# Reordering the second half of an attention and the distances behind it, token norms and root products on GpSimd, and row copies dealt out anew, in a decoder kernel on one Trainium2 core

## The chip, the cores and the metric

The kernel runs as one program on 1 core of a Trainium2 chip (trn2). The metric is device time in microseconds (us), the median of the timed runs. The engines are TensorE (PE in the profile), VectorE (DVE), ScalarE (ACT), GpSimd (POOL) and SyncE (SP), which only issues DMAs here.

## The reference

Two decoder layers over `x` of 8 sequences x 112 tokens x 256, with a context of 8 x 375 x 256. Each layer is self-attention, a cross step and a mixture of experts, each on a layer norm of `x` and added to it. The change lies in the first two steps of layer 0:

```python
x = x + _L0_attn_ref(_layernorm(x, axis=-1), Wk, Wq, Wv)     # causal, one head
x = x + _L0_xattn_ref(ctx_1024, _layernorm(x, axis=-1))
# in _L0_xattn_ref, for each of the 8 sequences (a: 375 context rows, b: 112 tokens):
#   D = sqrt(maximum(aa + bb - 2 * a @ b.T, 0))      aa, bb: sums of squares
#   R = dynamic time warping cost of D:  r = d + min(up, left, diagonal)
#   then the path is traced back through R, and the context rows on it are added to each token
```

## The kernel before

There is no scheduler: five instruction streams are written out by hand, one for each engine, and they meet in semaphores. T is 112 tokens, S 375 context rows, B 8 sequences; "pair q" is the sequences 2q and 2q+1, "half h" the sequences 4h to 4h+3. PSUM banks are handed out by a ring in the order of the `ring.take` calls, so a step can start only when the last reader of its bank has emptied it.

- **Attention, second half.** `shifted_scores(1)` on VectorE, `exp_rows(1, 0, 4)` on ScalarE (L1000), `weights_turned(1)` on TensorE (four transposes, L1216), `weights_moved(1)` on VectorE (L1818), `self_values(1)` on TensorE (L1213), `values_added(2)` and `(3)` on VectorE (L1826), which also take the statistics of the next layer norm. `ln_root` on GpSimd makes the reciprocal deviation `rstd` (L754, L755), `ln_norm(1, q)` on VectorE the normed tokens `N` (L1773).
- **What the distances need.** `ctx_turn(lo, hi)` on TensorE transposes the context into 12 banks, and `ctx_turned` on ScalarE copies them out (`ctxT_r`, L945). `pair_turn(turn1[q], 1, q)` transposes the normed tokens of a pair, `pair_turned` copies them out times -2 (`NT`, L945). `row_squares(q)` on ScalarE squares the normed tokens and sums them: `bb`, the token norms (L1014). The context norms lie in `root`.
- **Distances.** `distances(q)`: 4 products a sequence pair into two banks (`ps<-ctxT_r,NT`). `squares(lo, hi)` on VectorE adds the norms and empties the bank (L1837). `inverse_roots(lo, hi)` on ScalarE takes Relu, Ln and Exp(-0.5 x) (L1019 to L1021). `roots(n, lo, hi)` on VectorE (L1843 to L1845) takes the product z = d r and one Newton step, and signals `dist_ready`. There are five such groups n: sequences 0-1, 2-3, 4-5, 6 and 7.
- **Skewed copies.** The distances lie as [token, sequence, context column]; the recurrence wants them on 32 partitions, (g, b), where g is a quarter of the context columns. One DMA `skewed(b, g, k) <- plain_rows(b, g, k)` moves, for one sequence b and quarter g, the token rows of block k: rows 0-15 (k = 0), 16-47 (k = 1), 48-111 (k = 2), so 16, 32 or 64 rows of some 94 numbers. These are 96 DMAs, dealt by `mover` to the queues of SP (51, L627), ScalarE (19, L1058) and GpSimd (26, L797). Each waits for `dist_ready` of its sequence. GpSimd first clears the corners of the target (L780, L781: `dsk_clear`, for which SP and ScalarE wait), issues two loads of projection weights (`Wk`, `Wv`, L786), and clears the first cost rows (L791).
- **The recurrence.** 124 columns on VectorE, each with two scans (L1906) and two minima (L1901), with a shuffle (L1927) every third column. Before column q = 1, 5, 9 and 13 it waits for the first rows (k = 0) of quarter g = 0, 1, 2, 3 of all sequences, before column 17 for all of k = 1, before column 49 for all of k = 2. All that follows (path, experts, layer 1) hangs on its end.

## Time and profile before

| | |
|---|---|
| median of the 3 runs | 613.0 us (612.25 to 638.85) |
| profiled execution, its own time | 613.88 us |
| its span | 612.1 us |
| busy: PE, DVE, ACT, POOL | 469.0, 404.0, 222.1, 190.4 us |
| mean granted TensorE clock | 0.876 |

The span is what the rows below cover; the profiled execution's own time is 1.8 us longer. Times in rows are microseconds from the start of the span. An engine can be busy for most of the span and yet bound only some stages; so what counts is the chain of waits, stage by stage.

### The profile page before, as it was taken

The page shows a single profiled execution, that of the slowest core. Times are in us where ns is not written, and L with a number is a line of the kernel's source. Part 1 is how long each engine was busy: PE and PEld are TensorE (multiplying, and loading weights), DVE is VectorE, ACT ScalarE, POOL GpSimd, SP SyncE. Part 2 cuts the span into 40 slices and gives each one's busy share as a digit, 9 for nine tenths or more (in the row PEclk, how much of TensorE's full clock was granted, in tenths as well). Part 3 has the DMA queues.
Part 4 walks back from the last instruction along what each step waited for, and adds up shares of the span by engine and source line. Part 5 has one row for each costly group of instructions (what it writes and reads, how often), then busy time and mean ns, then how long its engine had stood idle before and what let it go on. Part 6 is the DMA issues. An engine that isn't in the chain of part 4 may idle for free.

```text
span 612.1 us, 9072 instructions
## 1 busy us (share of the span) xinstructions
PE 469.0 (77%) x2796; PEld 380.1 (62%) x2796; DVE 404.0 (66%) x1389; ACT 222.1 (36%) x670; POOL 190.4 (31%) x274
## 2 busy tenths in 40 slices
PE   7987799300030878799999989899998998799980
PEld 6975348200010346789999877788786775699850
DVE  6648569999899974715444376767764445756553
ACT  2546442200002324133444131779983353044300
POOL 6012630400000003156575227301103220377353
PEclk9988799755556899699999999979999996799995
DMA  9420298493100585222212230410007201155723
GB/s 231 85 90 2 54 52 36 92 110 64 18 0 5 170 303 169 91 71 70 69 60 63 75 82 0 123 52 2 2 1 222 88 2 60 35 150 169 130 84 114
DMA packets 49170, 50.43 MB, mean 82 GB/s; under 512 B 14768, under 2 KB 42052, under 8 KB 48900
## 3 DMA queue, kind: packets, MB, share of 16 engines
q1 hardware_dynamic: 40532, 34.53, 23.9%
q0 software_dynamic: 7824, 15.16, 11.4%
q8 instruction: 23, 0.38, 0.3%
q10 hardware_dynamic: 768, 0.18, 0.2%
q14 instruction: 23, 0.19, 0.1%
HBM read 37.48 MB, written 9.32 MB: 76 GB/s over the span
## 4 chain that ended last, share of the span: by engine, by line
PE 56%; DVE 26%; ACT 6%; DMA 4%; issue 3%; POOL 3%; ACTq 1%; POOLq 0%; DVEq 0%; SPq 0%
PE ps L1213 48%; DVE big L1906 8%; PE ps L1216 7%; DVE mtmp L1901 4%; POOL big L927 2%; DMA big<-Vc_r 2%; DVE big L2259 1%; ACT N_r L975 1%; ACTq L1058 1%; DVE rk L2251 1%; DVE big L1950 1%; DVE big L1951 1%; ACT big L945 1%; DVE big L1984 1%; DMA big<-in_L_attn_wo 1%
## 5 line engine op out<-in xcount | busy, mean ns | idle before, releaser
L1213 PE MATMUL ps<-ident 128*128 128x128 f32 (+1 forms) x304 | 63.0, 371 | 83.8 <-DVE big L1942 65.8
L1213 PEld LDWEIGHTS ps<-ident 128*128 128x128 f32 x304 | 45.4, 231 | 91.7 <-DVE big L1942 66.2
L1213 PE MATMUL ps<-ctxT_r,big 128*128 128x128 f32 (+1 forms) x616 | 82.8, 284 | 2.6 <-issue 1.1
L1213 PEld LDWEIGHTS ps<-ctxT_r,big 128*128 128x128 f32 (+1 forms) x616 | 75.8, 191 | 6.6 <-issue 4.3
L1906 DVE TENSOR_TENSOR_SCAN big<-mtmp,big 32x47 f32<-32x47 f32 x248 | 62.6, 287 | 8.1 <-DMA big<-Vc_r 8.1
L1213 PE MATMUL ps<-big 112*128 112x112 f32 (+6 forms) x458 | 63.2, 318 | 3.7 <-issue 3.4
L945 ACT ACTIVATE big<-ps 112x448 f32<-112x448 f32 (+6 forms) x65 | 38.2, 621 | 56.0 <-PE ps L1216 33.6
L1213 PEld LDWEIGHTS ps<-big 112*128 112x128 f32 (+5 forms) x458 | 53.0, 192 | 7.7 <-issue 4.4
L1216 PE MATMUL ps<-ident,big 112*112 112x112 f32 (+6 forms) x291 | 42.3, 285 | 13.0 <-DVE big L1984 4.4
L945 ACT ACTIVATE ctxT_r<-ps 128x256 f32<-128x256 f32 (+3 forms) x74 | 31.0, 433 | 57.2 <-PE ps L1216 47.0
L1216 PEld LDWEIGHTS ps<-ident,big 112*112 112x112 f32 (+6 forms) x291 | 32.3, 148 | 27.5 <-DVE big L1984 10.2
L1146 ACT ACTIVATE big<-ps,rk 112x112 f32<-112x112 f32 x128 | 43.9, 375 | 8.5 <-DVE rk L2252 8.0
L1213 PE MATMUL ps<-big,ctxT_r 128*128 x168 | 39.6, 380 | 0.0
L2194 DVE COPY big<-ps 128x256 f32<-128x256 f32 x21 | 8.9, 425 | 43.8 <-PE ps L1213 41.2
L918 POOL DMA_INDIRECT ctxT_r<-normed,source x29 | 32.5, 1119 | 15.6 <-PE ps L1216 8.8
L1901 DVE TENSOR_TENSOR mtmp<-big 32x47 f32<-32x47 f32 x246 | 37.1, 183 | 0.0
L754 POOL TENSOR_SCALAR veps<-mv 112x2 f32<-112x2 f32 x24 | 5.7, 238 | 99.2 <-DVE mv L1767 98.9
L1120 ACT ACTIVATE ctxT_r<-ps,big 128x128 f32<-128x128 f32 x84 | 23.9, 368 | 30.6 <-PE ps L1213 30.6
L1078 ACT ACTIVATE big<-big,ones 112x1500 f32<-112x1500 f32 x2 | 3.1, 1538 | 82.5 <-DVE big L1958 82.5
L1213 PEld LDWEIGHTS ps<-big,ctxT_r 128*128 128x128 f32 x168 | 30.4, 191 | 3.3
L846 POOL DMA_INDIRECT ctxT_r<-normed,source x21 | 25.5, 1217 | 21.0 <-PE ps L1216 12.9
L2251 DVE TENSOR_REDUCE rk<-ps 112x4 f32<-112x448 f32 x32 | 19.8, 620 | 17.2 <-PE ps L1213 17.2
(266 smaller groups left out, 941.5 us busy)
## 6 DMA issues: line engine op xcount, KB each, us to landing
big<-in_L_ffn_W SPq DMA_DIRECT2D x16, 512.0 KB, 6.9
routed<-Vc_r SPq DMA_DIRECT2D x29, 128.0 KB, 2.5
ctxT_r<-in_ctx POOLq DMA_DIRECT2D x4, 750.0 KB, 21.4
big<-in_ctx SPq DMA_DIRECT2D x4, 672.0 KB
big<-in_L_ffn_Wg SPq DMA_DIRECT2D x16, 128.0 KB, 2.5
big<-in_L_ffn_Wu SPq DMA_DIRECT2D x16, 128.0 KB, 2.6
big<-in_L_ffn_Wd SPq DMA_DIRECT2D x16, 128.0 KB, 2.5
normed<-N_r SPq DMA_DIRECT2D x2, 896.0 KB, 5.2
```

The lines of the kernel that those rows point to most:

```text
L846: pool.indirect_dma_start(out=Xg0[:, n % XR], out_offset=None, in_=normed0, in_offset=bass.IndirectOffsetOnAxis(ap=source[:, n:n + 1], axi ...
L918: pool.indirect_dma_start(out=Xg[:, n % XR], out_offset=None, in_=normed, in_offset=bass.IndirectOffsetOnAxis(ap=source[:, n:n + 1], axis= ...
L927: pool.indirect_dma_start(out=Yg[:, k * B + b], out_offset=None, in_=routed, in_offset=bass.IndirectOffsetOnAxis(ap=slot_id[:, k * B + b:k ...
L945: return nc.scalar.activation(dst, src, func, **kw).then_inc(free[act], 1)
L1120: ins = nc.scalar.activation(hT0[:, m % 2, j], src[:, j * 128:(j + 1) * 128], ACT.Relu, bias=b1t[:, j, m:m + 1])
L1146: ins = nc.scalar.activation(Px[:, n % NP, j * T:(j + 1) * T], bank(r_s1[n])[0:T, j * T:(j + 1) * T], ACT.Exp, bias=hm[:, n % NP, 1, j:j + ...
L1213: return nc.tensor.matmul(dst, lhsT, rhs, start=first, stop=last)
L1216: return nc.tensor.transpose(dst, src, ident[0:n, 0:n])
L1901: return step(v.tensor_tensor(mtmp[:, lo:hi], RS[:, q - 1, lo:hi], RS[:, q - 1, lo + 1:hi + 1], ALU.min))
L1906: return step(v.tensor_tensor_scan(RS[:, q, lo + 1:hi + 1], mtmp[:, lo:hi], Dsk[:, (q - 1) * RC + lo:(q - 1) * RC + hi], RS[:, q, lo:lo + ...
L2194: empty(r_y0[m], v.tensor_copy(yb0[:, m % YR], bank(r_y0[m])[:, 0:D]))
L2251: link(v.tensor_reduce(hm[:, n % NP, 0, :], src, AX_X, ALU.max))
```

## The change

It has four parts.

1. **Order** on TensorE and ScalarE (and the ring): the exponentials come ahead of two context copies; the context turns 4-5 and the turn of token pair 1 come ahead of the turned weights; token pairs 2 and 3 are turned ahead of `distances(2)` and `(3)`, which follow each other; `r_bias` goes last. On VectorE `squares(4, 6)` comes ahead of `roots(1, 2, 4)`.
2. **Token norms** `bb` are made on GpSimd as D x variance x rstd x rstd (three instructions on 112x2 a pair), in place of eight squares on ScalarE.
3. **Root product**: for groups n = 0, 1, 2 (`POOL_ROOTS = 3`) z = d r is one GpSimd instruction on 112x750; VectorE keeps the two others. ScalarE's Relu writes `Dd` in place.
4. **Copies**: a table `MOVES` deals the same 96 DMAs out as SP 53, GpSimd 31, ScalarE 12, in another order.

```diff
         MOVES = {
+            "sp": row_block(0, (0, 1), every) + row_block(0, (2, 3), every) + row_block(0, (4, 5), (0, 1))
+            + row_block(0, (6,), (0, 1)) + row_block(0, (7,), (0,)) + row_block(1, (4, 5), (1,))
+            + row_block(1, (6, 7), (0, 1)) + row_block(2, range(B), (0, 1, 2)),
...
+            "act": row_block(1, (2, 3), (0, 1)) + row_block(0, (7,), (1, 3)) + row_block(1, (2, 3), (2, 3))
+            + row_block(1, (4, 5), (0,))}
...
+            def row_squares(q4):
+
+                cols = slice(2 * q4, 2 * q4 + 2)
+                link(nc.gpsimd.tensor_scalar(bb[:, cols], mv[:, cols, 1], float(D), None, ALU.mult))
+                pool.wait_ge(s["rstd_ready"], B // 2 + q4 + 1)
+                link(nc.gpsimd.tensor_tensor(bb[:, cols], bb[:, cols], rstd[:, cols], ALU.mult))
+                nc.gpsimd.tensor_tensor(bb[:, cols], bb[:, cols], rstd[:, cols], ALU.mult).then_inc(s["bb_ready"], 1)
+
+            def first_product(n, lo, hi):
+                pool.wait_ge(s["inv_ready"], n + 1)
+                nc.gpsimd.tensor_tensor(root[:, lo:hi, :], Dd[:, lo:hi, :], inv[:, lo:hi, :], ALU.mult)\
+                    .then_inc(s["product_ready"], 1)
...
-            ln_root(1)
+            for q4 in range(B // 2):
+                ln_root(1, (q4,))
+                row_squares(q4)
+            if POOL_ROOTS:
+                first_product(0, 0, 2)
...
-            pool.wait_ge(s["bb_ready"], B)
...
+            for n in range(1, POOL_ROOTS):
+                first_product(n, 2 * n, 2 * n + 2)
+            for b, g, k in MOVES["pool"]:
...
             def roots(n, lo, hi):
                 d, r, z = Dd[:, lo:hi, :], inv[:, lo:hi, :], root[:, lo:hi, :]
-                ve.wait_ge(s["inv_ready"], n + 1)
-                link(v.scalar_tensor_tensor(z, d, 0.0, r, ALU.max, ALU.mult))
+                if n < POOL_ROOTS:
+                    ve.wait_ge(s["product_ready"], n + 1)
+                else:
+                    ve.wait_ge(s["inv_ready"], n + 1)
+                    link(v.tensor_tensor(z, d, r, ALU.mult))
```

On TensorE, from the turn of token pair 0 (`ident,N_r` is a turn of tokens, `ident,big` with 112x112 the turned weights and with 128x125 context turns, `ctxT_r,NT` a distance product, `big 112x256` the values). Before:

```order
L1216 MATMUL ps<-ident,N_r 128x112 x4
L1216 MATMUL ps<-ident,big 112x112 x4
L1216 MATMUL ps<-ident,big 128x125 x8
L1213 MATMUL ps<-ctxT_r,NT 112x375 x4
L1216 MATMUL ps<-ident,N_r 128x112 x4
L1213 MATMUL ps<-big 112x256 x4
L1213 MATMUL ps<-ctxT_r,NT 112x375 x4
L1216 MATMUL ps<-ident,big 128x125 x24
L1216 MATMUL ps<-ident,KcT_r 128x4
L1216 MATMUL ps<-ident,N_r 128x112 x4
L1213 MATMUL ps<-ctxT_r,NT 112x375 x4
L1216 MATMUL ps<-ident,N_r 128x112 x4
```

On the same engine from the same place, after the change:

```order
L1233 MATMUL ps<-ident,N_r 128x112 x4
L1233 MATMUL ps<-ident,big 128x125 x8
L1233 MATMUL ps<-ident,N_r 128x112 x4
L1233 MATMUL ps<-ident,big 112x112 x4
L1230 MATMUL ps<-ctxT_r,NT 112x375 x4
L1230 MATMUL ps<-big 112x256 x4
L1233 MATMUL ps<-ident,big 128x125 x16
L1230 MATMUL ps<-ctxT_r,NT 112x375 x4
L1233 MATMUL ps<-ident,N_r 128x112 x4
L1233 MATMUL ps<-ident,big 128x125 x8
L1233 MATMUL ps<-ident,N_r 128x112 x4
L1230 MATMUL ps<-ctxT_r,NT 112x375 x8
```

The last distances (the final x8) now stand behind both token turns in one piece, and nothing has to be turned and copied between them.

On GpSimd, from the last `rstd` of this layer norm to the first skewed copies. Before:

```order
L755 TENSOR_TENSOR rstd<-veps,mhalf 112x2
L780 MEMSET big 32x2x1128
L781 MEMSET big 32x100
L786 DMA N_r<-in_L_xattn_Wk 128x2x256
L786 DMA N_r<-in_L_xattn_Wv 128x2x256
L791 MEMSET big 32x475
L793 MEMSET big 8x1
L797 DMA big<-Vc_r 1x16x93 x8
```

And after the change:

```order
L763 TENSOR_TENSOR rstd<-veps,mhalf 112x2
L775 TENSOR_SCALAR bb<-mv 112x2
L777 TENSOR_TENSOR bb<-bb,rstd 112x2
L778 TENSOR_TENSOR bb<-bb,rstd 112x2
L782 TENSOR_TENSOR Vc_r<-Vc_r,big 112x750
L805 MEMSET big 32x2x1128
L806 MEMSET big 32x100
L810 DMA N_r<-in_L_xattn_Wk 128x2x256
L810 DMA N_r<-in_L_xattn_Wv 128x2x256
L815 MEMSET big 32x475
L817 MEMSET big 8x1
L782 TENSOR_TENSOR Vc_r<-Vc_r,big 112x750 x2
```

The first product stands ahead of the clearing of the copy's target, and the second and third behind the two loads and the clearing of the first cost rows; all of GpSimd's copies stand behind the third.

On the queue of SP, the skewed copies (a shape is sequences x rows x columns). Before:

```order
L627 DMA big<-Vc_r 1x16x94 x15
L627 DMA big<-Vc_r 1x32x94 x12
L627 DMA big<-Vc_r 1x64x94 x24
```

And after the change:

```order
L635 DMA big<-Vc_r 1x16x94 x6
L635 DMA big<-Vc_r 1x16x93 x2
L635 DMA big<-Vc_r 1x16x94 x6
L635 DMA big<-Vc_r 1x16x93 x2
L635 DMA big<-Vc_r 1x16x94 x7
L635 DMA big<-Vc_r 1x32x94 x6
L635 DMA big<-Vc_r 1x64x94 x24
```

SP now carries 23 copies of 16 rows and 6 of 32 rows ahead of the same 24 copies of 64 rows; the last of the 23 is sequence 7, quarter 0.

## Rows read from the trace of the kernel before

**Rows 1.** the page: its span, and the shares of the chain that ended last
```profile
span 612.1 us, 9072 instructions
...
PE 56%; DVE 26%; ACT 6%; DMA 4%; issue 3%; POOL 3%; ACTq 1%; POOLq 0%; DVEq 0%; SPq 0%
```

**Rows 2.** the chain of waits, 36 to 130 us: start, us, what
```profile
80.80 10.60 DMA big<-Vc_r
91.42 0.30 DVE big L1906
```

**Rows 3.** VectorE in order of time: start, us, instruction [idle before, what ended it]
```profile
47.12 0.88 DVE L1826 SCALAR_TENSOR_TENSOR X<-ps,rs,X 112x256 f32<-112x256 f32 x2 [0.64 <-PE ps L1213]
...
52.11 0.74 DVE L1773 TENSOR_SCALAR N_r<-X,mv,rstd 112x256 f32<-112x256 f32 x2 [0.60 <-POOL rstd L755]
...
54.77 0.94 DVE L1844 SCALAR_TENSOR_TENSOR big<-big,Vc_r 112x750 f32<-112x750 f32 x1
...
71.59 0.55 DVE L1845 SCALAR_TENSOR_TENSOR Vc_r<-big,Vc_r 112x375 f32<-112x375 f32 x1
...
75.72 0.30 DVE L1906 TENSOR_TENSOR_SCAN big<-mtmp,big 32x47 f32<-32x47 f32 x1 [3.47 <-DMA big<-Vc_r]
...
86.51 0.29 DVE L1906 TENSOR_TENSOR_SCAN big<-mtmp,big 32x47 f32<-32x47 f32 x1
```

**Rows 4.** TensorE in order of time, the same columns
```profile
40.31 2.66 PE L1216 MATMUL ps<-ident,big 112*112 112x112 f32 x12 [2.32 <-ACT big L1000]
...
50.30 2.73 PE L1216 MATMUL ps<-ident,big 125*128 125x125 f32 x24
...
57.09 4.44 PE L1213 MATMUL ps<-ctxT_r,NT 128*112 128x375 f32 x8 [2.55 <-ACT NT L945]
...
62.59 2.75 PE L1213 MATMUL ps<-ctxT_r,NT 128*112 128x375 f32 x8 [0.68 <-ACT NT L945]
```

**Rows 5.** a stretch: us, busy of each engine, granted clock (PEclk), DMA share, GB/s
```profile
58.00:59.00 1.00, 1.00 (x2) 0.37 (x2) 0.97 (x2) 0.00 (x0) 0.00 (x0) 0.50 0.06 12
```

**Rows 6.** ScalarE in order of time
```profile
48.34 0.92 ACT L1020 ACTIVATE big<-big,tiny 112x750 f32<-112x750 f32 x1
...
50.93 2.98 ACT L945 ACTIVATE ctxT_r<-ps 128x500 f32<-128x500 f32 x6 [0.81 <-PE ps L1216]
...
61.95 0.54 ACT L945 ACTIVATE NT<-ps 128x448 f32<-128x448 f32 x1 [4.17 <-PE ps L1216]
...
104.07 4.51 ACT L945 ACTIVATE Vc_r<-ps 125x512 f32<-125x512 f32 x9 [11.86 <-DMA big<-Vc_r]
```

**Rows 7.** GpSimd in order of time
```profile
53.09 1.97 POOL L780 MEMSET big<- 32x2256 f32 x1 [1.01 <-PE ps L1216]
...
64.61 0.72 POOL L786 DMA_DIRECT2D N_r<-in_L_xattn_Wv  x1
...
72.43 9.36 POOL L797 DMA_DIRECT2D big<-Vc_r  x19 [1.14 <-DVE Vc_r L1845]
```

**Rows 8.** GpSimd, groups by shape: busy us, mean ns of one
```profile
L866 POOL TENSOR_TENSOR X<-X,big 112x2048 f32<-112x2048 f32 x2 | 9.2, 4586 | 3.2 <-ACT N_r L975 3.2
L894 POOL TENSOR_TENSOR big<-big 128x448 f32<-128x448 f32 x8 | 7.4, 930 | 6.7 <-DVE big L2246 6.7
L852 POOL TENSOR_TENSOR ctxT_r_split<-big,ctxT_r_split 128x256 fp32r<-128x256 f32 x6 | 6.5, 1084 | 2.8 <-ACT ctxT_r_split L1125 2.7
```

**Rows 9.** SP's queue issuing DMAs, 56 to 63 us
```profile
56.77 5.69 SPq L627 DMA_DIRECT2D big<-Vc_r  x9
```

**Rows 10.** ScalarE's copies issued from 73.1 us, then from 79.5 us, and their landing
```profile
L1058 ACTq DMA_DIRECT2D big<-Vc_r x3: 600/600/616, 73.1 to 74.4; - x3
...
DMA to landing us min/median/max: 2.6/2.7/2.7
...
L1058 ACTq DMA_DIRECT2D big<-Vc_r x3: 601/603/608, 79.5 to 80.8; - x3
...
DMA to landing us min/median/max: 7.2/8.8/10.6
```

More of the change, by code:

```diff
@@ L527, in decoder_kernel @@
         first_rows_moved = [sem(f"first_cost_rows_moved{g}") for g in range(G)]
+        pool_first_rows_moved = [sem(f"first_cost_rows_moved_by_pool{g}") for g in range(G)]
         rows_moved = {k: sem(f"cost_rows_moved{k}") for k in range(1, NBLK)}
@@ L560, in plain_rows, with row_block, first_rows_in, pool_row_sem @@
             return bass.AP(src.tensor, src.offset, [src.ap[0], [1, min(RC, S - g * RC)]])
-        def mover(b, g, k):
-            if g == G - 1:
-                return "pool"
-            if k == 0:
-                return "act" if b in (3, 5, 7) else "sp"
-            if k == 1:
-                return ("sp", "sp" if b < HB else "act", "act" if b < B - 2 else "pool")[g]
-            return "sp"
-        def moved_by(queue, k):
-            pairs = [(b, g) for q4 in range(B // 2) for g in range(G) for b in (2 * q4, 2 * q4 + 1)]
-            return [(b, g) for b, g in pairs if mover(b, g, k) == queue]
+        def row_block(k, bs, gs):
+            return [(b, g, k) for g in gs for b in bs]
+        every = range(G)
+        MOVES = {
+            "sp": row_block(0, (0, 1), every) + row_block(0, (2, 3), every) + row_block(0, (4, 5), (0, 1))
+            + row_block(0, (6,), (0, 1)) + row_block(0, (7,), (0,)) + row_block(1, (4, 5), (1,))
+            + row_block(1, (6, 7), (0, 1)) + row_block(2, range(B), (0, 1, 2)),
+            "pool": row_block(1, (0, 1), every) + row_block(0, (4, 5), (2, 3)) + row_block(0, (6,), (2, 3))
+            + row_block(0, (7,), (2,)) + row_block(1, (4, 5), (2, 3)) + row_block(1, (6, 7), (2, 3))
+            + row_block(2, range(B), (3,)),
+            "act": row_block(1, (2, 3), (0, 1)) + row_block(0, (7,), (1, 3)) + row_block(1, (2, 3), (2, 3))
+            + row_block(1, (4, 5), (0,))}
+        assert sorted(sum(MOVES.values(), [])) == [(b, g, k) for b in range(B) for g in every for k in range(NBLK)]
         def rows_in(k):
-            n = len(moved_by("pool", k))
+            n = sum(move[2] == k for move in MOVES["pool"])
             return 16 * (G * B - n), 16 * n
+        def first_rows_in(g):
+            n = sum(move[1:] == (g, 0) for move in MOVES["pool"])
+            return 16 * (B - n), 16 * n
         def row_sem(k, g):
             return first_rows_moved[g] if k == 0 else rows_moved[k]
+        def pool_row_sem(k, g):
+            return pool_first_rows_moved[g] if k == 0 else pool_rows_moved[k]
         def step_of(seg, g):
@@ L623, in _ @@
             sp.wait_ge(s["dsk_clear"], 1)
-            for k in range(NBLK):
-                for b, g in moved_by("sp", k):
-                    sp.wait_ge(s["dist_ready"], max(b // 2, b - 3) + 1)
-                    sp.dma_start(skewed(b, g, k), plain_rows(b, g, k)).then_inc(row_sem(k, g), 16)
+            for b, g, k in MOVES["sp"]:
+                sp.wait_ge(s["dist_ready"], max(b // 2, b - 3) + 1)
+                sp.dma_start(skewed(b, g, k), plain_rows(b, g, k)).then_inc(row_sem(k, g), 16)
             sp.wait_ge(s["edge_ready"], 1)
@@ L1034, in _ @@
             norms_turned(1)
+            exp_rows(1, 0, 4)
             ctx_turned(2, 4)
             pair_turned(turn1[0], 0, scale=-2.0)
[L1037 to L1038 removed]
             ctx_turned(4, 6)
             pair_turned(turn1[1], 1, scale=-2.0)
[L1041 removed]
             inverse_roots(0, 2)
[L1043 to L1044 removed]
+            ctx_turned(6, 10)
+            pair_turned(turn1[2], 2, scale=-2.0)
+            ctx_turned(10, 12)
+            pair_turned(turn1[3], 3, scale=-2.0)
             inverse_roots(2, 4)
[L1046 to L1049 removed]
             inverse_roots(4, 6)
@@ L1052, in _ @@
             inverse_roots(7, 8)
+            copy(r_bias, bcol[:, :], bank(r_bias)[:, 0:NB])
             sc.wait_ge(s["dsk_clear"], 1)
-            for k in range(2):
-                for b, g in moved_by("act", k):
-                    sc.wait_ge(s["dist_ready"], max(b // 2, b - 3) + 1)
-                    sc.dma_start(skewed(b, g, k), plain_rows(b, g, k)).then_inc(row_sem(k, g), 16)
+            for b, g, k in MOVES["act"]:
+                sc.wait_ge(s["dist_ready"], max(b // 2, b - 3) + 1)
+                sc.dma_start(skewed(b, g, k), plain_rows(b, g, k)).then_inc(row_sem(k, g), 16)
             sc.wait_ge(free[act], r_bias.count)
@@ L1879, in _ @@
             roots(0, 0, 2)
+            squares(4, 6)
             roots(1, 2, 4)
-            squares(4, 6)
             squares(6, 7)
```

71 lines of the change are left out of this document (31 added, 40 removed).

## Prediction

> **What bounds the kernel now.** First the page's shares of the chain that ended last: TensorE 56%, VectorE 26% [rows 1]. This says nothing of the changed stage, so I read the chain of waits from 36 to 130 us. The change ends where the recurrence on VectorE begins. From there the chain is VectorE alone, column after column, with one hole: a copy issued at 80.80 us on ScalarE's queue lands 10.60 us later, at 91.4, and a scan starts with it [rows 2]. VectorE in order of time shows both debts of the old order. The last distance is done at 71.59 + 0.55 = 72.1, and the first scan starts at 75.72, 3.47 us idle behind a copy. Then 16 columns run until 86.51 + 0.29 = 86.8, and column 17 starts at 91.42: 4.62 us idle [rows 3, 2]. From 75.72 to 86.80, 16 columns take 11.08 us, 0.69 each. Behind column 17 nothing waits until column 49 and further: ScalarE's value copies, which wait for all blocks, went on at 104.07 [rows 6], and column 49 comes at 91.42 + 32 x 0.69 = 113.5. Whatever starts column 17 earlier therefore moves the rest of the kernel by as much; the later stages wait for each other and for loads that this chain releases.
>
> Before 72.1 the old order loses time in three places. TensorE waits 2.32 us for the exponentials and then runs its turns slowly (12 in 2.66 us, where 24 take 2.73 later) [rows 4]. It waits 2.55 us for a token copy and then takes 4.44 us for eight distance products, where the next eight take 2.75 [rows 4]: the granted clock there is 0.50 [rows 5]. And VectorE has nine root steps behind the last distance bank.
>
> **The change, laid end to end with those durations.** I start at 37.4, where nothing has moved yet.
>
> *Order.* ScalarE's two context copies and one token copy, 2 x 0.49 + 0.44 = 1.4 us [rows 6], no longer stand ahead of the exponentials, so these end at 38.9 instead of 40.3. TensorE meanwhile turns two context banks (0.46 each, 2.73 / 6 [rows 4]) and a token pair, until 39.2, and then the weights. Its idle of 2.32 shrinks to some 0.7 before distances(0), which start at 40.4 when ScalarE has made up the 1.4. With 2.8 a distance pair (2.75 [rows 4]) and 1.8 for the values: distances(0) end at 43.2, values 45.0, four context banks 46.8, distances(1) 49.7, token pair 2, two banks and pair 3 at 51.4, distances(2) and (3) together at 57.1. Before, the last ended at 62.59 + 2.75 = 65.3. The x update of pair 2 starts at 44.2 in place of 47.12, and the norm of pair 3 (52.11 before [rows 3]) at 49.05.
>
> *Norms.* Eight squares leave ScalarE. GpSimd gets 3 small instructions a pair, some 0.8 us with their links; for pairs 2 and 3 they end at 48.0 and 49.8, beside VectorE's work. The squares step needs them later: nothing.
>
> *Product.* No row shows a GpSimd product of 112x750. Two float32 ones give 930 / 448 = 2.1 and 4586 / 2048 = 2.2 ns an element, the one that rounds its output 1084 / 256 = 4.2 [rows 8]. So the bounds are 1.6 and 3.2 us; I take 1.65, the shape and type being those of the first two. It takes 0.94 (a VectorE step [rows 3]) off VectorE three times, 2.8 us, but GpSimd's line is in order. Product 0 runs 49.8 to 51.4; then the two clearings (1.97 [rows 7] and 0.28) to 53.65, which frees SP's copies; the two load issues (1.5, the second 0.72 [rows 7]) and the clearing of cost rows (0.67) to 55.8. The second root factor of ScalarE (three steps, 2.6 us, the middle one 0.92 [rows 6]) is ready at 54.6. So product 1 runs 55.8 to 57.5, over a second late, and VectorE stands idle for 2.7 us before its two steps: group 1 is done at 59.45. Product 2 runs 57.6 to 59.2 and delays nobody. VectorE: squares of 6 and 7 to 60.5, group 2 to 62.4, 3 to 64.1, 4 to 65.75. The last distance is thus done 6.4 us before 72.1.
>
> *Copies.* SP issues nine 16-row copies in 5.69 us, 0.632 each [rows 9]. Its first eight run from 53.65 to 58.7. The other eight of pairs 0 and 1 wait for group 1, 59.5; from there 14 stand ahead of (7, quarter 0), which is issued at 59.5 + 14 x 0.632 = 68.3, 2.6 us after its distance is ready. SP's queue, not VectorE, then starts the recurrence, and what sets SP is product 1. Before, ScalarE issued that copy at 73.1, and it landed after 2.6 [rows 10], at 75.7: the first scan. So now 68.3 + 2.6 = 70.9: **4.8 us earlier**.
>
> The second debt: the rows of k = 1 are issued by 72.1 on SP (6 behind 68.9), 70.2 on GpSimd, 70.1 on ScalarE, where the last one went out at 80.8. Copies issued from 73.1 landed in 2.6 to 2.7 us; those of 79.5 to 80.8 took 7.2 to 10.6 [rows 10]. Between lie GpSimd's 64-row copies: its 19 from 72.43 on are 11 shorter and then 8 of those [rows 7], so the first went at 77.85. SP's last one now goes 1.4 us after GpSimd's first of 64 rows (70.7); before, 1.65 us after it the price was 7.2. So it lands by 79.3. Column 17 comes at 70.9 + 11.1 = 82.0 and finds it there, with 2.7 us to spare: **4.6 us saved**. k = 2 is issued to 88.8 and at 10.6 us a landing lies there by 99, against column 49 at 104. ScalarE, free at 71.4 instead of 81.4, copies keys earlier; TensorE's key and value products ended well before the recurrence and are off the path.
>
> Sum: 4.8 + 4.6 = 9.4 us. SP and ScalarE will issue together from 63.7, with which I charge a single stall of 0.3, leaving 9.1. The profiled execution took 613.88 (a span of 612.1 and 1.8 around it), so 604.8; the median lies 0.9 lower: **603.9**.
>
> **The rivals.**
>
> *Product dear.* While product 2 runs, VectorE has its two steps of group 1 in hand, with both operands in the same memory. The Trainium skill ("SBUF — State Buffer", Who interferes with whom) holds that a VectorE instruction with two SBUF inputs and a GpSimd one that reads SBUF exclude each other, the second waiting for the whole of the first. No row here shows that; at 1.65 us it would cost 0.6 us at the last distance, all inside the 2.6 that SP is late, so the sum would be the same by rule or without. At 3.2 us a product with the two taking turns: product 0 puts 1.55 on all behind it, product 1 as much, and product 2, first in turn, holds VectorE's steps back 3.1 to 3.2 more. Group 1 is then 6.2 us later, SP with it, and 9.4 - 6.2 = 3.2 are left: 609.8. Without turns 5.1 - 6.0 are left. For it: 4.2 ns is on record for a GpSimd instruction. Against: the two of its own type. Chance 0.14.
>
> *The hole stays.* SP's last k = 1 copy may pay 10.6 or more instead of 7, since at that time GpSimd's eight 64-row copies and SP's own come behind each other closer than before. At 10.6 it lands at 82.7 and costs 0.7; if the whole hole stays, 4.8 are left, 608.2. Chance 0.12.
>
> *Slower than before.* One mechanism: the product on GpSimd, with turns. Each further us of product puts 3 to 4 us on group 1; 9.4 us are eaten at 3.2 + 3.2 / 3.5 = 4.1 us or a little above. At 5 us (6.7 ns an element) it would be 3 us slower, 616. No row of such shape comes near: 0.04.
>
> *It does not do what it says.* SP's queue of 53, or the copies of k = 2, hold column 49 in place of 17: it has 5 us of cover. If used up and more, 3 are lost: 607. Chance 0.05.
>
> *More gained.* With a product at 1.2, or clearings that start sooner, group 1 comes at 58.5 and the scan at 69.9: 10.4 saved, 602.6. To pass 2% (12.3 us) SP would have to be ready at 65, before the last distance. Chance 0.08, of which 0.03 beyond 2%.
>
> **How the numbers follow.** The forecast has 0.57 and spans 602.6 to 605.5, with half a microsecond either way for another run. The range takes in the dear product and the kept hole: 602.0 to 610.2. About 2% (12.3 us) is what a measurement of this kernel tells from no change. By the cases: faster by more 0.04, within 0.93, slower 0.03.
>
> **What would show it.** In the changed profile: distances in one piece of 16 products ending near 57 at full clock; a GpSimd row of 112x750 of some 1650 ns; VectorE idle some 2.7 us in front of its first step of group 1, waiting for GpSimd; the first scan near 71, released by a copy of SP's queue; no idle time before column 17 (near 82). It is wrong if the product is over 2 us, if VectorE's steps stretch beside it, or if column 17 or 49 waits for a copy.

## The result, and the profile after

The changed kernel takes **605.18 us** (median of 4 runs, 603.93 to 606.38), forecast 603.9. Beside it the kernel before took 612.25 and 613.0; two further runs of it (638.65 and 638.85) and some of most kernels below, among them the profiled ones of e3, e5 and e6, were in a slower state and are left out of every ratio. The ratio is 0.9878, 95% interval [0.9831, 0.9926]: some 7.4 us faster, less than 2% at its middle. The profiled execution took 604.03 us. The page of after, its span and the shares of the chain that ended last (TensorE down, VectorE up in share):

```profile
span 602.1 us, 9072 instructions
...
PE 49%; DVE 30%; POOL 5%; DMA 5%; ACT 5%; issue 4%; SPq 1%; POOLq 0%; DVEq 0%
```

The two profiled executions are not level where the change begins. In a stretch of 4 us (length, busy time of PE, granted clock, DMA share, GB/s), before:

```profile
12.00:16.00 4.00, 3.56 (x10) 0.60 1.12 232
```

and after:

```profile
12.00:16.00 4.00, 3.61 (x17) 1.00 1.11 238
```

TensorE had the lower of its two levels (1.2 of 2.4 GHz) for most of that stretch in before alone. To take differences ahead of the change out I count from **P**, the end of the norm of token pair 1 on VectorE, the last step that no kernel here moves. VectorE of before, that norm (P = 37.15 + 0.73 = 37.88) and the last scan of the recurrence:

```profile
37.15 0.73 DVE L1773 TENSOR_SCALAR N_r<-X,mv,rstd 112x256 f32<-112x256 f32 x2
...
165.44 0.30 DVE L1906 TENSOR_TENSOR_SCAN big<-mtmp,big 32x47 f32<-32x47 f32 x1
```

VectorE of after, in order of time (P = 36.47):

```profile
35.74 0.73 DVE L1791 TENSOR_SCALAR N_r<-X,mv,rstd 112x256 f32<-112x256 f32 x2
...
50.47 0.94 DVE L1865 SCALAR_TENSOR_TENSOR big<-big,Vc_r 112x750 f32<-112x750 f32 x1 [1.07 <-POOL Vc_r L782]
...
56.38 2.50 DVE L1865 SCALAR_TENSOR_TENSOR big<-big,Vc_r 112x750 f32<-112x750 f32 x1 [2.97 <-POOL Vc_r L782]
58.91 0.94 DVE L1866 SCALAR_TENSOR_TENSOR Vc_r<-big,Vc_r 112x750 f32<-112x750 f32 x1
...
65.41 0.55 DVE L1866 SCALAR_TENSOR_TENSOR Vc_r<-big,Vc_r 112x375 f32<-112x375 f32 x1
...
71.85 0.30 DVE L1927 TENSOR_TENSOR_SCAN big<-mtmp,big 32x47 f32<-32x47 f32 x1 [5.79 <-DMA big<-Vc_r]
...
156.91 0.30 DVE L1927 TENSOR_TENSOR_SCAN big<-mtmp,big 32x47 f32<-32x47 f32 x1
```

The last distance is done at P + 29.5 (P + 34.3 before), the first scan starts at P + 35.4 (P + 37.8 [rows 3]), the last at P + 120.4 (P + 127.6). From first to last scan it is 89.7 before and 85.1 after: the 4.62 us of [rows 2] are gone. So by these two executions the change is worth **7.1 us** at the end of the recurrence; the rest of the 10 us between the spans lies in other stages and in P. VectorE stood idle 2.97 us for product 1 and then took 2.50 us for a step that takes 0.94.

TensorE, GpSimd, and the chain of waits:

```profile
38.93 2.75 PE L1230 MATMUL ps<-ctxT_r,NT 128*112 128x375 f32 x8 [0.76 <-ACT NT L970]
...
49.10 5.21 PE L1230 MATMUL ps<-ctxT_r,NT 128*112 128x375 f32 x16
```

```profile
48.65 1.79 POOL L782 TENSOR_TENSOR Vc_r<-Vc_r,big 112x750 f32<-112x750 f32 x1
50.38 1.97 POOL L805 MEMSET big<- 32x2256 f32 x1
...
54.59 3.49 POOL L782 TENSOR_TENSOR Vc_r<-Vc_r,big 112x750 f32<-112x750 f32 x2
...
66.25 8.41 POOL L822 DMA_DIRECT2D big<-Vc_r  x17 [0.35 <-DVE Vc_r L1866]
```

```profile
68.16 0.61 SPq L635
68.81 3.02 DMA big<-Vc_r
```

TensorE's idle of 2.32 is down to 0.76, and the 4.44 us for eight products [rows 4] are gone; distances 2 and 3 are one piece at full clock. Products take 1.75 to 1.79 us. Product 1 and product 2 stand back to back in one row, 54.59 to 58.08. The first scan waits for SP's queue: (7, quarter 0), its 23rd copy, was issued at 68.81, 2.85 us behind the last distance. GpSimd's 17 copies from 66.25 on are nine shorter ones and then eight of 64 rows, the first of these at 70.7.

Counting from P doesn't take out everything. In before the granted clock fell once more behind P; here are the 2 us in which the first turns ran (same columns as above):

```profile
40.00:42.00 2.00, 1.69 (x9) 0.53 0.81 279
```

These twelve turns took 2.66 us [rows 4]. The kernel of e1 below has the same instructions in the same order up to the last distance, and the same idle time in front; at a granted clock of 1.00 it took

```profile
38.84 1.45 PE L1223 MATMUL ps<-ident,big 112*112 112x112 f32 x12 [2.32 <-ACT big L1006]
```

With the eight products behind (3.06 and 2.69 us) this makes the 1.6 us by which its last distance comes earlier (P + 32.7). So up to 1.6 us of the 4.8 at the last distance, and with it of the 7.1, belong to one execution's clock and not to the change. The 4.44 us are another matter: behind an idle time of 2.56 us (2.55 before) the eight products took 4.25 in e1 too, with a granted clock of 0.50 from 56 to 58 us; that loss goes with the old order; in the changed kernel the clock stays at 1.00 from 36 to 60 us.

### The profile page after: what moved, and what is told of

Read it like the earlier page. It is cut to its first block, busy times and chain, and to the rows that moved or that the text cites. A ratio compares the mean times of both kernels' runs of the same rounds, so it can differ in the third digit from the quotient of the medians.

```text
span 602.1 us, 9072 instructions
## 1 busy us (share of the span) xinstructions
PE 458.8 (76%) x2796; PEld 371.8 (62%) x2796; DVE 402.8 (67%) x1386; ACT 218.8 (36%) x654; POOL 201.6 (33%) x294
## 4 chain that ended last, share of the span: by engine, by line
PE 49%; DVE 30%; POOL 5%; DMA 5%; ACT 5%; issue 4%; SPq 1%; POOLq 0%; DVEq 0%
PE ps L1230 43%; DVE big L1927 9%; PE ps L1233 7%; DVE mtmp L1922 4%; POOL big L952 2%; DVE big L2283 1%; DVE rk L2275 1%; ACT N_r L1000 1%; DVE big L1974 1%; DVE big L1975 1%; ACT big L970 1%; DMA big<-in_L_attn_wo 1%; DVE big L2008 1%; DMA big<-scattered 1%; DVE big L1951 1%
## 5 line engine op out<-in xcount | busy, mean ns | idle before, releaser
L1230 PE MATMUL ps<-ident 128*128 128x128 f32 (+1 forms) x304 | 60.6, 361 | 76.6 <-DVE big L1966 58.4
L1230 PEld LDWEIGHTS ps<-ident 128*128 128x128 f32 x304 | 43.3, 221 | 84.4 <-DVE big L1966 58.8
L1230 PE MATMUL ps<-big 112*128 112x112 f32 (+6 forms) x458 | 60.4, 308 | 3.7 <-issue 3.4
L970 ACT ACTIVATE big<-ps 112x448 f32<-112x448 f32 (+6 forms) x65 | 38.6, 627 | 54.3 <-PE ps L1233 34.3
L1230 PEld LDWEIGHTS ps<-big 112*128 112x128 f32 (+5 forms) x458 | 50.8, 184 | 7.8 <-issue 4.3
L970 ACT ACTIVATE ctxT_r<-ps 128x256 f32<-128x256 f32 (+3 forms) x74 | 31.1, 432 | 52.5 <-PE ps L1233 25.9
L1233 PE MATMUL ps<-ident,big 112*112 112x112 f32 (+6 forms) x291 | 40.6, 275 | 11.7 <-DVE big L2008 4.4
L1233 PEld LDWEIGHTS ps<-ident,big 112*112 112x112 f32 (+6 forms) x291 | 30.7, 143 | 25.7 <-DVE big L2008 10.2
L1000 ACT ACTIVATE N_r<-X,shift,rstd 112x256 f32<-112x256 f32 x32 | 17.4, 592 | 36.0 <-POOL shift L769 36.0
```

Of the source, the lines that this page charges most:

```text
L970: return nc.scalar.activation(dst, src, func, **kw).then_inc(free[act], 1)
L1000: nc.scalar.activation(N[:, b, :], X[:, b, :], ACT.Identity, bias=shift[:, b:b + 1], scale=rstd[:, b:b + 1]).then_inc(s["norm_ready"], 1)
L1230: return nc.tensor.matmul(dst, lhsT, rhs, start=first, stop=last)
L1233: return nc.tensor.transpose(dst, src, ident[0:n, 0:n])
```

## The experiments

All read in one table. Times are P + the number, each from one profiled execution; landing is that of (7, quarter 0) after its issue; "hole" is idle time before column 17. The ratio is to before on the same chip; its intervals are 2 to 6 us either way, and every one of them overlaps the changed kernel's (those of e2 and e10 barely), so the times don't rank these kernels. The traces repeat better: kernels with the same work up to the last distance have it within 0.3 us (changed and e7; e4, e5, e8 and e11), the 1.6 us between before and e1 apart. And in all fourteen traces the last scan comes 85.0 to 85.2 us behind the first, plus the hole. So only two numbers have to be explained, the first scan and the hole. From 36 to 60 us the mean granted clock was 0.87 in before, 0.93 in e1 and e6, and 0.99 or 1.00 in all others.

| kernel | last distance | (7, q0) issued, landing | first scan | hole | last scan | ratio, 95% |
|---|---|---|---|---|---|---|
| before | 34.3 | 35.2, 2.6 | 37.8 | 4.6 | 127.6 | 1 |
| changed | 29.5 | 32.3, 3.0 | 35.4 | 0 | 120.4 | 0.9878 [0.9831, 0.9926] |
| e1_copies_only | 32.7 | 34.2, 2.8 | 37.0 | 0 | 122.1 | 0.9869 [0.9773, 0.9965] |
| e2_copies_undone | 29.5 | 30.6, 3.0 | 33.6 | 4.3 | 123.0 | 0.9961 [0.9917, 1.0005] |
| e3_product2_later | 28.9 | 31.3, 3.1 | 34.4 | 0 | 119.5 | 0.9870 [0.9835, 0.9905] |
| e4_one_product | 26.8 | 31.6, 6.4 | 38.0 | 0 | 123.0 | 0.9899 [0.9843, 0.9954] |
| e5_hold_big | 26.6 | 31.1, 2.6 | 33.7 | 0 | 118.7 | 0.9874 [0.9829, 0.9919] |
| e6_norms_back | 30.8 | 33.6, 3.0 | 36.7 | 0 | 121.7 | 0.9909 [0.9879, 0.9939] |
| e7_sp_order | 29.2 | 29.4, 2.2 | 31.6 | 3.0 | 119.7 | 0.9915 [0.9879, 0.9951] |
| e8_best | 26.8 | 28.2, 2.7 | 30.9 | 0 | 115.9 | 0.9860 [0.9810, 0.9909] |
| e9_order_only | 27.6 | 27.8, 1.9 | 29.8 | 4.5 | 119.3 | 0.9906 [0.9855, 0.9957] |
| e10_norms_back_guarded | 29.2 | 32.0, 2.8 | 34.8 | 0 | 119.8 | 0.9967 [0.9919, 1.0016] |
| e11_front | 26.8 | 26.9, 2.1 | 29.0 | 0 | 114.1 | 0.9815 [0.9747, 0.9883] |
| e12_products_back | 26.6 | 30.3, 2.8 | 33.1 | 1.8 | 120.0 | 0.9936 [0.9889, 0.9982] |

### e1_copies_only: the kernel before with the new table

```diff
-            for k in range(NBLK):
-                for b, g in moved_by("sp", k):
...
+            for b, g, k in MOVES["sp"]:
```

(Part of the edit; the same for the queues of GpSimd and ScalarE, and the table)

> The old order, norms and roots, with the new table of copies alone. All times are counted from P, the end of the norm of token pair 1 on VectorE (37.88 us in the profile before, 36.47 in that of the change), so that a slower or faster start does not count. Before: first scan at P + 37.8, column 17 at P + 53.5, last scan at P + 127.6. Changed: P + 35.4, P + 46.5, P + 120.4, that is 7.1 us earlier. Theory (two separate debts): copies alone do not move the first scan by more than 0.6 us (it needs the last distance and, after it, one copy), but close the hole before column 17: idle there below 0.3 us in place of 4.6, last scan at P + 122.6 to 123, 607.5 to 608.5 us in all. Rival (the hole closes only because the order frees ScalarE early and SP can start early): idle before column 17 stays at 2 us or more, and the total within 2 us of before.

The chain and VectorE at the first scan:

```profile
70.66 2.79 DMA big<-Vc_r
```

```profile
73.47 0.30 DVE L1913 TENSOR_TENSOR_SCAN big<-mtmp,big 32x47 f32<-32x47 f32 x1 [4.24 <-DMA big<-Vc_r]
```

The hole is gone, and the last scan comes 5.5 us earlier than before: 4.6 of the hole and 0.8 at the first scan, more than the 0.6 allowed for, where the last distance came 1.6 us earlier by the clock. The table by itself closes the hole.

### e2_copies_undone: the changed kernel with the old dealing

```diff
-            for b, g, k in MOVES["sp"]:
+            for k in range(NBLK):
+                for b, g in moved_by("sp", k):
```

(Part of the edit; the same for the queues of GpSimd and ScalarE)

> The changed kernel with the old table of copies (SP 51, GpSimd 26, ScalarE 19). Theory: the first scan comes at P + 33.5 to 34.5, a little sooner than the P + 35.4 of the change, since sequence 7's first copy is then 7th on ScalarE's queue, free at 63.9 us; but the hole before column 17 is back with 4 to 6 us, because ScalarE's last 32-row copy goes out 3.5 us behind GpSimd's first 64-row one. Last scan P + 123.5 to 125, total 3 to 4.5 us slower than the change, 608 to 610. Rival (the order alone is what helps): no hole, total as the change or 1 us faster.

ScalarE, and VectorE in order of time:

```profile
64.92 0.52 ACT L1032 ACTIVATE Vc_r<-Vc_r 112x375 f32<-112x375 f32 x1 [4.30 <-DVE Vc_r L1848]
```

```profile
60.90 2.50 DVE L1858 SCALAR_TENSOR_TENSOR big<-big,Vc_r 112x750 f32<-112x750 f32 x1 [2.96 <-POOL Vc_r L775]
...
74.61 0.30 DVE L1920 TENSOR_TENSOR_SCAN big<-mtmp,big 32x47 f32<-32x47 f32 x1 [4.02 <-DMA big<-Vc_r]
...
89.98 0.30 DVE L1920 TENSOR_TENSOR_SCAN big<-mtmp,big 32x47 f32<-32x47 f32 x1 [4.29 <-DMA big<-Vc_r]
```

The hole is back with 4.29 us, and the last scan is 2.6 us later than in the changed kernel, although the first is 1.8 us earlier. The 2.50 us step is there again.

### e3_product2_later: product 2 only behind group 1

```diff
             for n in range(1, POOL_ROOTS):
+                if n == 2:
+                    pool.wait_ge(s["dist_ready"], 2)
                 first_product(n, 2 * n, 2 * n + 2)
```

> The changed kernel, with one wait more: GpSimd takes the third product only when the distances of group 1 are done. Theory (VectorE and GpSimd exclude each other while both read two operands): in the profile of the change VectorE's first step of group 1 took 2.50 us in place of 0.94, beside product 2; here it takes 0.94, group 1 is done 1.5 us earlier, and so are SP's copy of sequence 7, the first scan (P + 33.9) and the last scan (P + 118.9): 1.5 us faster than the change, though product 2 itself comes 1.9 us later. Rival (the 2.50 is something else, such as a late hand-over or DMA work of GpSimd): the step stays over 2 us, and the total does not move or is slower.

```profile
57.34 0.94 DVE L1867 SCALAR_TENSOR_TENSOR big<-big,Vc_r 112x750 f32<-112x750 f32 x1 [2.94 <-POOL Vc_r L782]
```

With nothing else on GpSimd the same step takes 0.94 in place of 2.50 (so it does in e4, at 55.61), and group 1 is done at P + 21.8 in place of P + 23.4. At the first scan 1.0 of these 1.6 us is left: the first of SP's copies behind group 1 (59.3) took 0.9 us in place of 0.6, and the landing and GpSimd's line did not move with it. So product 2 beside VectorE's step costs about 1 us at the end of the recurrence; the times, 0.9870 and 0.9878, don't show it.

### e4_one_product: `POOL_ROOTS = 1`

```diff
-        POOL_ROOTS = 3
+        POOL_ROOTS = 1
```

> The changed kernel with one root product on GpSimd in place of three (POOL_ROOTS = 1): groups 1 and 2 take their product on VectorE. Theory (product 1 came late because it stands behind clearings and loads on GpSimd): VectorE has group 1 done at 56.3 in place of 59.9, SP's copy of sequence 7 goes out 3.5 us earlier, at about 65, right behind the last distance at 63.7; first scan P + 31.5 to 32, last scan P + 117, 3.5 us faster than the change, 601.5 us. Rival (taking 0.94 us three times off VectorE is what makes the change fast): the last distance comes later than the 65.9 of the change and the kernel is slower by 1 to 2 us.

The chain, and GpSimd:

```profile
69.36 6.36 DMA big<-Vc_r
```

```profile
64.90 8.42 POOL L822 DMA_DIRECT2D big<-Vc_r  x17 [0.35 <-DVE Vc_r L1866]
```

The last distance comes 2.7 us earlier, and the first scan 2.6 us **later**. My expectation of the issue was also wrong in its sum: SP had 22 copies of 0.63 ahead of (7, quarter 0), from 53.9 on and without a pause, which is 67.8, and one of them took 1.6. It came at 69.36, just as GpSimd's first 64-row copy went (64.90 + 9 x 0.495 = 69.35), and then landed after 6.36 us.

### e5_hold_big: e4 with the 64-row copies held

```diff
-        POOL_ROOTS = 3
+        POOL_ROOTS = 1
...
+            held = True
...
+                if k == 2 and held:
+                    pool.wait_ge(first_rows_moved[0], first_rows_in(0)[0])
+                    held = False
```

> The kernel with one GpSimd product, in which GpSimd also holds its copies of k = 2 (64 rows each) until the first rows of quarter 0 have all landed. It is compared with the one-product kernel, whose first scan stood at P + 38.0 and last scan at P + 123.0 (P: the end of the norm of token pair 1 on VectorE), and where the copy of (7, quarter 0) was issued at P + 31.6 and landed after 6.36 us. Theory (GpSimd's 64-row copies in flight stretched that landing): it lands after 2.6 to 3.2 us, the first scan stands at about P + 34.5, the last at about P + 119.5, 3.4 us earlier than there; of times, about 602.5. Rival (the landing is long because SP's own 22 copies were issued without a pause ahead of it): it stays over 5 us and the first scan within 1 us of P + 38.

```profile
68.89 2.58 DMA big<-Vc_r
```

The landing is 2.58 us, and the last scan 4.3 us earlier than in e4 (of 3.4 expected). So GpSimd's 64-row copies in flight stretched the landing, and not SP's own line.

### e6_norms_back: token norms on ScalarE again

```diff
-                row_squares(q4)
...
+            pool.wait_ge(s["bb_ready"], B)
...
+            row_squares(0)
```

> The changed kernel with the token norms on ScalarE as before (eight squares with a sum; GpSimd waits for all of them ahead of its two loads), all else as changed. Theory (ScalarE has 1.1 and 4.3 us idle in that stage, and the three small GpSimd instructions a pair cost GpSimd's line 0.8 us ahead of product 0): no more than 0.8 us either way, first scan at P + 34.6 to P + 36, so that the move of the norms is worth nothing by itself. Rival (ScalarE's second and third root factors come later by its squares, four of 0.4 us): the group-1 step comes 1.6 us or more later, first scan at P + 37, and the time is 1.6 us or more above the changed kernel.

VectorE, GpSimd and TensorE in order of time:

```profile
49.50 4.01 DVE L1793 TENSOR_SCALAR N_r<-X,mv,rstd 112x256 f32<-112x256 f32 x1 [0.60 <-POOL rstd L763]
```

```profile
49.43 1.81 POOL L774 TENSOR_TENSOR Vc_r<-Vc_r,big 112x750 f32<-112x750 f32 x1
51.17 1.97 POOL L796 MEMSET big<- 32x2256 f32 x1
```

```profile
53.97 0.57 PE L1235 MATMUL ps<-ident,N_r 112*128 112x112 f32 x4 [3.19 <-DVE N_r L1793]
```

1.3 us later at the last scan than the changed kernel, beyond the 0.8 of the theory; but not by the rival's mechanism. The norm of one sequence of pair 3 took 4.01 us, where such a norm takes 0.4: it began 0.07 behind product 0 and ended 0.37 behind the clearing. TensorE waited 3.19 us for it, and behind that wait its granted clock was 0.50 (56 to 58 us) and distances 2 and 3 took 6.90 us in place of 5.21. In the changed kernel the three small norm instructions put product 0 at 48.65, 0.3 us behind the last of these norms (48.36).

### e7_sp_order: SP's list by readiness

```diff
-            "sp": row_block(0, (0, 1), every) + row_block(0, (2, 3), every) + row_block(0, (4, 5), (0, 1))
-            + row_block(0, (6,), (0, 1)) + row_block(0, (7,), (0,)) + row_block(1, (4, 5), (1,))
+            "sp": row_block(0, (0, 1), every) + row_block(0, (2, 3), (0, 1)) + row_block(0, (2,), (2,))
+            + row_block(0, (4, 5), (0,)) + row_block(0, (3,), (2,)) + row_block(0, (6,), (0,)) + row_block(0, (2,), (3,))
+            + row_block(0, (7,), (0,)) + row_block(0, (4, 5), (1,)) + row_block(0, (6,), (1,)) + row_block(0, (3,), (3,))
+            + row_block(1, (4, 5), (1,))
```

> The changed kernel with nothing but SP's list in another order: the 16-row copies of quarter 0 go as soon as their distance is there, (7, quarter 0) right at the last distance instead of behind 14 copies that are ready with group 1, and the copies of quarters 1 to 3 fill in between and behind. Same copies on the same queues. Theory (SP's line in front of (7, quarter 0) sets the first scan): it is issued at P + 29.6 to 30, lands after 2.6, first scan at about P + 32.4 (changed kernel: P + 35.4), last scan at about P + 117.5; with column 17 at P + 43.5 and the last copy of k = 1 landed by P + 42.5. About 3 us faster than the changed kernel, 602. Rival 1 (the last distance or something else sets it): first scan within 1 us of P + 35.4. Rival 2 (the end of k = 1 is late in its place): idle time before column 17 of 1 to 3 us and no gain at the last scan.

```profile
72.23 9.78 DMA big<-Vc_r
```

```profile
82.04 0.30 DVE L1929 TENSOR_TENSOR_SCAN big<-mtmp,big 32x47 f32<-32x47 f32 x1 [3.00 <-DMA big<-Vc_r]
```

The first scan comes 3.8 us earlier, so SP's line did set it. Then rival 2: SP's last copy of k = 1, issued at 72.23 among the 64-row copies, lands after 9.78, and column 17 waits 3.00. Of 3.8 us 0.7 is left, not the 3 expected; the ratio, 0.9915, shows no gain at all.

### e8_best: one product, and a table for both terms

```diff
+            "pool": row_block(1, (0, 1), every) + row_block(0, (2, 3), (3,)) + row_block(1, (2, 3), (2, 3))
+            + row_block(0, (4, 5), (2, 3)) + row_block(0, (6,), (2, 3)) + row_block(0, (7,), (2,))
+            + row_block(1, (4, 5), (2, 3)) + row_block(1, (6, 7), (2, 3)) + row_block(2, range(B), (3,)),
+            "act": row_block(1, (2, 3), (0, 1)) + row_block(1, (4, 5), (0,)) + row_block(0, (7,), (1, 3))
+            + row_block(1, (6, 7), (1,))}
```

(Part of the edit; with `POOL_ROOTS = 1`. SP's list is that of e11, below, with the two copies of quarter 2 ahead of (7, quarter 0).)

> One GpSimd product (last distance 2.7 us earlier than in the changed kernel) and a new table of copies: SP's list in the order in which distances come ready, some copies of quarters 1 to 3 given from SP to ScalarE and GpSimd. Theory (both terms together, SP's line and GpSimd's 64-row copies in flight, set the first scan): (7, quarter 0) is issued at P + 27.6, first scan at about P + 30.5, last scan at about P + 115.5, 5 us faster than the changed kernel, about 600. Rival (the copies then come so close that k = 1 lands late): idle time of over 1 us in front of column 17, and a last scan at P + 117 or later.

```profile
65.91 2.68 DMA big<-Vc_r
```

No hole, last scan at P + 115.9: 4.5 us earlier than the changed kernel. SP's last copy of k = 1 is issued at 70.4 here, 0.2 us behind GpSimd's first 64-row copy, and lands in 4.5.

### e9_order_only: the new order and nothing else

```diff
-        POOL_ROOTS = 3
+        POOL_ROOTS = 0
...
-            for b, g, k in MOVES["sp"]:
+            for k in range(NBLK):
+                for b, g in moved_by("sp", k):
```

(Part of the edit, against the changed kernel; the other queues in the same way, and the norms on ScalarE as in e6. Of part 3 it keeps that Relu writes `Dd` in place and that VectorE's product is a `tensor_tensor`.)

> The new order of the second half alone: token norms on ScalarE, all root products on VectorE and the copies as before. To be read beside the kernel before (last distance P + 34.3, first scan P + 37.8, last scan P + 127.6; P is the end of the norm of token pair 1) and beside the changed kernel with the old copies (P + 29.5, P + 33.6, P + 123.0). Theory (of what the change wins ahead of the copies, all is the order; moving the product and the norms to GpSimd adds nothing): last distance at P + 27 to P + 28, first scan at P + 31 to P + 32.5, the hole before column 17 still there with 4 to 6 us, last scan at P + 121 to P + 123. Rival (ScalarE's squares hold up the root factors, so that the norms on GpSimd are what lets the order pay): last distance at P + 29.5 or later and the last scan at P + 124 or later.

ScalarE, and VectorE:

```profile
58.76 0.52 ACT L1030 ACTIVATE Vc_r<-Vc_r 112x375 f32<-112x375 f32 x1 [0.94 <-DVE Vc_r L1850]
```

```profile
67.41 0.30 DVE L1922 TENSOR_TENSOR_SCAN big<-mtmp,big 32x47 f32<-32x47 f32 x1 [2.01 <-DMA big<-Vc_r]
...
82.96 0.30 DVE L1922 TENSOR_TENSOR_SCAN big<-mtmp,big 32x47 f32<-32x47 f32 x1 [4.46 <-DMA big<-Vc_r]
```

The order alone starts the recurrence 8.1 us earlier and ends it 8.2 us earlier than before (up to 1.6 us of either by the clock in before's trace), 1.1 us **ahead of the whole change**, with the hole still in it. That is better than I expected. Beside e2, which adds the products and norms on GpSimd, it starts 3.9 us earlier. That is the price of those moves together, with the old dealing: ScalarE waits 4.30 us in e2, and 0.94 here, for the squares that stand behind group 1 on VectorE; its own copies, (7, quarter 0) its seventh, then start at P + 26.8 in place of P + 24.0, and (7, quarter 0) lands in 3.0 in place of 1.9. (Order alone ahead of the whole change is read from one execution of each; the ratios, 0.9906 and 0.9878, don't part them.)

### e10_norms_back_guarded: e6, and product 0 behind the norms

```diff
+                pool.wait_ge(s["norm_ready"], 2 * B)
                 first_product(0, 0, 2)
```

(Part of the edit; the rest is e6's edit)

> The kernel with the norms back on ScalarE, and one more wait: GpSimd starts product 0 only when VectorE has normalised token pair 3. Without it the first of these two norms took 4.01 us (0.40 elsewhere) beside GpSimd's product 0 (1.81) and clearing (1.97), and the first scan stood at P + 36.65. Theory (that norm and GpSimd's instructions exclude each other, which is what made the norms on ScalarE dearer): the norm takes 0.4 again, TensorE's distances 2 and 3 run in one piece of 5.2 us, and the first scan stands at P + 35 to P + 35.8, as in the changed kernel. Rival (the 1.3 us come from ScalarE's squares): the norm takes 0.4, the first scan stays at P + 36.3 or later.

VectorE, and GpSimd:

```profile
48.49 0.74 DVE L1794 TENSOR_SCALAR N_r<-X,mv,rstd 112x256 f32<-112x256 f32 x2 [0.60 <-POOL rstd L763]
...
57.99 2.40 DVE L1869 SCALAR_TENSOR_TENSOR Vc_r<-big,Vc_r 112x750 f32<-112x750 f32 x1
```

```profile
57.62 1.97 POOL L774 TENSOR_TENSOR Vc_r<-Vc_r,big 112x750 f32<-112x750 f32 x1 [0.64 <-ACT big L1039]
```

A wait added makes it 1.9 us faster than e6 in the trace (first and last scan alike): both norms take 0.74 together. The stretched step is now the other one of group 1, 2.40, since product 2 starts later. It starts at 57.62, while VectorE's first step (57.02, 0.94 us) still runs, and is stretched itself, to 1.97. The times don't repeat the gain: they point the other way (0.9967 beside 0.9909, on different chips, with intervals that overlap). So the mechanism rests on the rows, and that the kernel as a whole gains is not shown.

### e11_front: e8 with (7, quarter 0) first of all

```diff
-            + row_block(0, (2,), (2,)) + row_block(0, (6,), (0,)) + row_block(0, (3,), (2,)) + row_block(0, (7,), (0,))
-            + row_block(0, (4, 5), (1,)) + row_block(0, (6,), (1,)) + row_block(1, (4, 5), (1,))
+            + row_block(0, (6,), (0,)) + row_block(0, (7,), (0,))
+            + row_block(0, (4, 5), (1,)) + row_block(0, (6,), (1,)) + row_block(0, (2, 3), (2,)) + row_block(1, (4, 5), (1,))
```

> The kernel with one product and the new table (first scan P + 30.86, last scan P + 115.9; its copy of (7, quarter 0) was SP's 18th, issued 1.3 us after the last distance behind two copies of quarter 2), with these two copies of quarter 2 moved behind the quarters 0 and 1. Theory (what stands ahead of (7, quarter 0) on SP still sets the first scan): it is issued at P + 26.9, first scan at P + 29.6, last scan at P + 114.6, 1.3 us faster, about 601 us. Rival (quarter 2 is late for column 9, or a long landing): idle time of 0.5 us or more before column 5, 9 or 17 and the last scan where it was.

```profile
65.63 2.13 DMA big<-Vc_r
```

```profile
67.78 0.30 DVE L1928 TENSOR_TENSOR_SCAN big<-mtmp,big 32x47 f32<-32x47 f32 x1 [2.07 <-DMA big<-Vc_r]
```

It is issued 0.03 us behind the last distance; no column waits later. The last scan comes 6.3 us ahead of the changed kernel's, the earliest here, and the ratio, **0.9815**, is the lowest, though its interval overlaps the changed kernel's.

### e12_products_back: `POOL_ROOTS = 0` in the changed kernel

```diff
-        POOL_ROOTS = 3
+        POOL_ROOTS = 0
```

> The changed kernel with all root products on VectorE (0.94 each) and none on GpSimd; order, norms and copies as changed. It stands beside the kernel with one product there (last distance P + 26.8, first scan P + 38.0, last scan P + 123.0). Theory (the first product on GpSimd wins and costs nothing, since VectorE stands 1.07 us waiting for it, and what sets the first scan is SP's line and GpSimd's 64-row copies in flight): last distance within 0.5 us of P + 26.8, the landing of (7, quarter 0) 5 us or more, first scan at P + 37 to P + 38.5, last scan at P + 122 to P + 123.5, which is 2 to 3 us later than with three products on GpSimd. Rival (VectorE's line sets it): first scan at P + 32 or less.

```profile
71.56 11.79 DMA big<-Vc_r
```

```profile
83.37 0.30 DVE L1927 TENSOR_TENSOR_SCAN big<-mtmp,big 32x47 f32<-32x47 f32 x1 [1.76 <-DMA big<-Vc_r]
```

The last distance came as expected, the landing and both scans did not, and neither did the rival's first scan (P + 32 or less): SP began 0.3 us earlier against P than in e4, lost 1 us less on long issues, and issued (7, quarter 0) at 67.73, 1.0 ahead of GpSimd's first 64-row copy (64.34 + 9 x 0.49 = 68.8), and it landed in 2.8. Then SP's last k = 1 copy paid 11.79, and column 17 waited. In sum P + 120.0, level with the changed kernel (P + 120.4): the three products on GpSimd win nothing. At the last distance they lose: 26.6 without a product there, 26.8 with one, 29.5 with three.

## Why the prediction was right, and where not

**What held.** The direction and, roughly, the size: 9.1 us forecast, 7.1 measured at the last scan and 7.4 (4.5 to 10.4) in the times. The order on TensorE and ScalarE came out as laid end to end (idle of 0.7 forecast, 0.76 measured; distances 2 and 3 in one piece). SP's queue, not VectorE, starts the recurrence, 2.6 us behind the last distance forecast, 2.85 measured. VectorE's idle of 2.7 for product 1 was 2.97. The hole closed, 4.6 forecast, 4.66 measured between the scans; e1 and e2 show that the table of copies does it. Columns 17 and 49 wait for nothing.

**The step that failed:** "Product 2 runs 57.6 to 59.2 and delays nobody", with the exclusion priced at 0.6 us "all inside the 2.6 that SP is late". In its place the runs showed a stall of 1.56 us. Product 2 was not behind VectorE's step but ahead of it: the products ran back to back, and the first step of group 1 took 2.50 in place of 0.94. Those 1.56 us are not in SP's slack, because the fourteen copies in front of (7, quarter 0) start with eight that wait for group 1 itself: the slack lay behind that point. e3 removes it and gets 1.0 us at the end. The row came first; the Trainium skill ("SBUF — State Buffer", 🔬 SBUF: two separate sides) has the rule, a VectorE operation with two SBUF inputs against a GpSimd one that reads SBUF, the one that starts first keeping the port for its whole length. The traces agree: 2.50 beside product 2, 0.94 beside the clearing, which reads nothing (50.47 beside 50.38), and 0.94 alone; in e10, where VectorE's step was first, that took 0.94 and the product 1.97.

**Terms mis-sized.** Product 1.75 to 1.79, forecast 1.65: 0.2 to 0.3 on two of them ahead of group 1. Landing 3.0, forecast 2.6. With 1.56 these make 2.2 of the 2.4 us by which the first scan came later against P than forecast (P + 33.0, from 70.9 in a trace with P at 37.88). The price of SP's last k = 1 copy, 7.2 by a copy of ScalarE's queue, was 9.7; that cost nothing here, but it used up most of the room, see below.

**Booked on the wrong account.** The turns that before "runs slowly" (12 in 2.66 us) were counted as a debt of the old order. The same order in e1 ran them in 1.45. So 1.6 us of what was forecast for the last distance, and of what was measured there, is the clock of one execution: forecast and measurement both hold it because both are read against the same trace, and that part of their agreement is luck; no run here shows how often a run of the kernel before pays it.

**Credited to the wrong part.** The sum of 4.8 for the first scan took order, norms and products as one. By e9 the order alone is worth 8.1 there, with up to 1.6 of it the clock; products and norms on GpSimd take 3.9 back (e2), and the table another 1.8 while it saves the 4.3 of the hole. It is products 1 and 2 that cost, 2.7 us at the last distance (e4 beside the changed kernel); product 0 moves it by 0.2 at most. The norms' move cost nothing: without products the last distance comes 1.0 us earlier with it (e12 beside e9, where VectorE waits 0.95 for ScalarE's root factor), with three there is no such gain (e10, 29.2 beside 29.5). The 0.94 taken "off VectorE three times" never reached the end, since GpSimd's line is in order and product 1 stands behind clearings and loads. The order alone and the table alone (e1, P + 122.1) each bring most of the gain, and they don't add: beside the order, the rest of the change wins nothing at the last scan (120.4 against 119.3). The order with the new table and all else as before was not run; e12, with the norms on GpSimd besides, comes nearest (P + 120.0).

**What the rivals were.** "Product dear" did not come by price but by turn. "The hole stays" did not happen here, but did in e7 and e12, where column 17 would have come earlier without the wait (P + 42.7 and P + 44.2 in place of P + 46.5): SP's last k = 1 copies landed in 9.8 and 11.8 us, not 7. In the changed kernel two of them, issued at 72.0 and 72.6, landed in

```profile
DMA to landing us min/median/max: 9.0/9.3/9.7
```

so by 82.3, against column 17 at 82.9: 0.6 us to spare, where I had forecast 79.3 and 2.7.

**Open.** What follows the last scan took 446.7 us in the trace of before and 445.2 in that of the changed kernel, and from 443.7 (e12) to 447.8 (e9) in the others without e3, e5 and e6; no run here says why. So the 7.1 us of one pair of traces and the 7.4 of the times agree only as far as that.
